# Two inner layers whose Gelu stays in its PSUM bank, with three smaller moves of order, in a macaron block with a long convolution

## The reference

```python
def _L0_ffn_ref(x, ...):                       # weights w1, w2, h1, h2, w3 hold -1, 0 or 1
    h = silu(_tlin(x, w1_w, w1_s)) * _tlin(x, w2_w, w2_s)      # 256 -> 1024
    h = gelu(_tlin(h, h1_w, h1_s), approximate=False)          # 1024 -> 1024
    h = gelu(_tlin(h, h2_w, h2_s), approximate=False)          # 1024 -> 1024
    return _tlin(h, w3_w, w3_s)                                # 1024 -> 256
...
x = x + 0.5 * ffn(layernorm(x))
x = x + attn(layernorm(x))                     # y = gelu(causal convolution with taps K); y @ W.T + b
x = x + 0.5 * ffn(layernorm(x))
```

## Time and profile before

| | us |
|---|---|
| median of 3 runs | 1358.97 (1357.96 to 1359.03) |
| profiled execution, own time | 1357.48 |
| its span in the trace | 1355.7 |
| PE busy | 1318.3 (97%) |
| DVE busy | 922.8 (68%) |
| ACT busy | 759.2 (56%) |
| POOL busy | 419.8 (31%) |

### The profile page before, as it was taken

One profiled execution on the slowest core, in us unless ns is written; L12 is line 12 of the kernel. 1 busy time (PEld: TensorE's weight loads), 2 busy tenths in 40 slices (PEclk: granted clock), 3 DMA queues, 4 the chain that ended last, 5 costly groups with the idle time before them and its releaser, 6 DMA issues.

```text
span 1355.7 us, 18622 instructions
## 1 busy us (share of the span) xinstructions
PE 1318.3 (97%) x7278; PEld 669.2 (49%) x7278; DVE 922.8 (68%) x1742; ACT 759.2 (56%) x1201; POOL 419.8 (31%) x354
## 2 busy tenths in 40 slices
PE   8999879999999999999999999999999999999997
PEld 3454344555544435455454554545545455454544
DVE  5376978832544886888878888789877883454723
ACT  5565247564447457474674746747467464545533
POOL 6822861200010442625326253262532610001000
PEclk9999989999999999999999999999999999999999
DMA  8210000000010000000000000000000002131400
GB/s 332 95 47 9 8 1 10 8 1 16 0 47 17 0 16 1 8 9 0 10 7 9 8 16 9 24 9 8 16 8 24 8 11 76 44 113 37 150 1 18
DMA packets 44703, 41.90 MB, mean 31 GB/s; under 512 B 32704, under 2 KB 41408, under 8 KB 41920
## 3 DMA queue, kind: packets, MB, share of 16 engines
q1 hardware_dynamic: 44608, 40.64, 10.0%
HBM read 28.57 MB, written 4.19 MB: 24 GB/s over the span
## 4 chain that ended last, share of the span: by engine, by line
PE 80%; DVE 15%; ACT 3%; issue 1%; DMA 1%; POOL 0%; SPq 0%; DVEq 0%; ACTq 0%; POOLq 0%
PE psf L1327 52%; PE psf L1315 14%; PE psf L1339 8%; DVE arena L786 4%; DVE hab L616 3%; DVE arena L789 3%; PE pss L1390 2%; PE pss L1400 2%; PE pss L1380 1%; PE pss L1355 1%; DVE xnp L675 1%; DVE arena L242 1%; PE pss L1370 1%; ACT ht L1098 1%; DVE arena L783 0%
## 5 line engine op out<-in xcount | busy, mean ns | idle before, releaser
L1327 PE MATMUL psf<-hab,wall 128*128 128x512 f16 x4096 | 893.0, 380 | 8.8 <-DVE hab L616 4.8
L1327 PEld LDWEIGHTS psf<-hab,wall 128*128 128x128 f16 x4096 | 399.1, 98 | 492.0 <-issue 9.3
L616 DVE SCALAR_TENSOR_TENSOR hab<-ht,hab 128x512 f16<-128x512 f32 x384 | 317.3, 831 | 286.8 <-ACT hab L1090 283.7
L1098 ACT ACTIVATE ht<-psf,scf 128x512 f32<-128x512 f32 x256 | 174.3, 681 | 411.0 <-PE psf L1327 398.7
L1090 ACT ACTIVATE hab<-ht 128x512 f16<-128x512 f32 x384 | 241.4, 629 | 28.8 <-DVE ht L627 20.4
L1315 PE MATMUL psf<-h,wall 128*128 128x512 f16 x1024 | 233.7, 381 | 17.8 <-ACT sil L1080 16.6
L1315 PEld LDWEIGHTS psf<-h,wall 128*128 128x128 f16 x1024 | 99.5, 98 | 135.4 <-ACT sil L1080 18.5
L954 POOL TENSOR_SCALAR rs<-mv 128x4 f32<-128x4 f32 x16 | 6.2, 389 | 493.7 <-DVE mv L658 487.5
L627 DVE SCALAR_TENSOR_TENSOR ht<-psf,scf,sil 128x512 f32<-128x512 f32 x128 | 95.9, 750 | 81.8 <-PE psf L1315 73.1
L1080 ACT ACTIVATE sil<-psf,scf 128x512 f32<-128x512 f32 x128 | 88.0, 687 | 86.0 <-PE psf L1315 83.9
L1339 PE MATMUL psf<-wall,hab 128*128 128x256 f16 x1024 | 117.0, 273 | 0.0
(11 more groups left out here) (127 smaller groups left out, 873.4 us busy)
## 6 DMA issues: line engine op xcount, KB each, us to landing
arena<-wh SPq DMA_DIRECT2D x8, 1024.0 KB, 5.5
g<-wh SPq DMA_DIRECT2D x6, 1024.0 KB, 10.1
out<-xr SPq DMA_DIRECT2D x15, 256.0 KB, 2.2
xr<-x SPq DMA_DIRECT2D x7, 512.0 KB, 5.1
arena<-w SPq DMA_DIRECT2D x3, 1024.0 KB, 5.3
g<-w SPq DMA_DIRECT2D x2, 1024.0 KB, 6.8
xr<-wh SPq DMA_DIRECT2D x2, 1024.0 KB, 10.3
g<-w SPq DMA_DIRECT2D x2, 512.0 KB, 6.1
```

What stands on the lines that cost most here:

```text
L616: e.scalar_tensor_tensor(out=hab[:, buffer(p), m, 1, :], in0=ht[:, p % 3, :], scalar=2.0 ** E2 if l else 1.0, in1=hab[:, buffer(p), m, 0, ...
L1098: e.activation(ht[:, p % 3, :], psf[bank_use(i, "hid", s) % MAIN][:, :], ACT.Gelu, scale=scf[:, 2 + l, m:m + 1]).then_inc(s_gelu, 1)
L1327: ins = e.matmul(bank[:, :], WH[:, l, m // 2, k, ms], hab[:, buffer(p), k, part, :], start=(k == 0 and part == 0), stop=(k == KH - 1 and p ...
```

## The change

There are five edits. (1) Gelu of an inner tile is written back to its own bank, and both splits read the bank; `ht` serves the gate's tiles alone. The bank is free for PE when the low half is done. (2) Tile 15 is split like the others, ahead of the first Silu and the first gate. (3) The factors' cast on ACT stands in slot 25 of pass 1, their low half on DVE in slot 7 of pass 2 (due from slot 3); four of the rounds of matmuls that use them, and the casts around them, move by two or three slots. (4) The bias is added by DVE in slot 14. (5) `BESIDE` is cut in slot 6 from 2700 to 2000 and in slot 14 from 2700 to 1500; `halves` is cut into pieces.

```diff
-BIAS_AT = 12
+BIAS_AT = 14
-BESIDE = [0, 500, 2000, 2700, 2700, 2700, 2700, 6800] + [0, 500, 2000, 2700, 2700, 2700, 2700, 1000]
+BESIDE = [0, 500, 2000, 2700, 2700, 2700, 2000, 6800] + [0, 500, 2000, 2700, 2700, 2700, 1500, 1000]
+FACTORS_HIGH_AT, FACTORS_LOW_AT = T(1, 25), T(2, 3)
@@ bank_free
             if s < 16:
-                return s_gelu, 2 * KH * i + s + 1
+                return s_lo, tile(i, 1, s) + 1
@@
+        def source(p):
+            i, s = divmod(p, 3 * KH)
+            return ht[:, (KH * i + s) % 3, :] if s < KH else psf[bank_use(i, "hid", s - KH) % MAIN][:, :]
@@ dve_program
-                    out=hab[:, buffer(p), m, 1, :], in0=ht[:, p % 3, :], scalar=2.0 ** E2 if l else 1.0,
+                    out=hab[:, buffer(p), m, 1, :], in0=source(p), scalar=2.0 ** E2 if l else 1.0,
@@
+            def bias_rows(b):
+                rows = xr[:, NB * b:NB * (b + 1), :]
...
+                e.tensor_tensor(rows, rows, bb[:, :].unsqueeze(1).to_broadcast([P, NB, D]), ALU.add).then_inc(s_xb, 1)
+                return 2300
@@
-                for s in range(2 * KH - 1):
+                for s in range(2 * KH):
                     split_low(tile(i, 1, s))
                     slot(i, s)
...
-                    behind = tile(i, 1, 2 * KH - 1)
+                    behind = tile(i + 1, 0, 0)
@@ act_program
-                w.wait_ge(s_lo, p - 2)
-                e.activation(ht[:, p % 3, :], psf[bank_use(i, "hid", s) % MAIN][:, :], ACT.Gelu,
-                             scale=scf[:, 2 + l, m:m + 1]).then_inc(s_gelu, 1)
+                e.activation(bank, bank, ACT.Gelu, scale=scf[:, 2 + l, m:m + 1]).then_inc(s_gelu, 1)
@@
-                yield At(mark["pj"][0] + 1)
+                yield At(FACTORS_HIGH_AT)
```

More of the change, by code:

```diff
@@ L624, in gate @@
                 w.wait_ge(s_silu, KH * i + m + 1)
-                if p >= 3:
-                    w.wait_ge(s_lo, p - 2)
+                g = KH * i + m - 3
+                if g >= 0:
+                    w.wait_ge(s_lo, tile(g // KH, 0, g % KH) + 1)
                 e.scalar_tensor_tensor(
-                    out=ht[:, p % 3, :], in0=psf[bank_use(i, "up", 2 * m + 1) % MAIN][:, :], scalar=scf[:, 1, m:m + 1],
+                    out=source(p), in0=psf[bank_use(i, "up", 2 * m + 1) % MAIN][:, :], scalar=scf[:, 1, m:m + 1],
                     in1=sil[:, m % 2, :], op0=ALU.mult, op1=ALU.mult).then_inc(s_gate, 1)
@@ L708, in taps, with factors_low @@
                 mark["pj"] = now["slot"], ch.n
-                yield At(now["slot"] + 1)
+            def factors_low():
+                yield At(FACTORS_LOW_AT)
                 for q in range(2):
@@ L722, in powers @@
                         yield time
-                    k = halves(ch, 1, n)
-                    yield 2 * (cost(qh[1][0][0]) + quick(qh[1][0][0]))
-                    mark["qlo", n] = now["slot"], k
+                    if not n:
+                        yield from factors_low()
+                    for time in halves(ch, 1, n):
+                        mark["qlo", n] = now["slot"], ch.n
+                        yield time
             def taps_low():
@@ L863, in fixed @@
                         time += y_low(u)
+                    if u % 2 and s == BIAS_AT:
+                        time += bias_rows(u // 2)
                     for half in range(2):
@@ L921, in dve_program @@
                 else:
-                    split_low(tile(i, 1, 2 * KH - 1))
-                    slot(i, 2 * KH - 1)
                     assert strand.over
@@ L989, in powers @@
                         yield 2.2 * time
-                    k = halves(ch, 0, n)
-                    yield 9000
-                    pmark["qlo", n] = now["slot"], k
+                    for time in halves(ch, 0, n):
+                        pmark["qlo", n] = now["slot"], ch.n
+                        yield 2.2 * time
             def first_products(u):
@@ L1089, in split_high @@
                     w.wait_ge(s_gate, KH * i + m + 1)
-                e.activation(hab[:, buffer(p), m, 0, :], ht[:, p % 3, :], ACT.Copy,
+                e.activation(hab[:, buffer(p), m, 0, :], source(p), ACT.Copy,
                              scale=2.0 ** E2 if l else 1.0).then_inc(s_hi, 1)
```

33 lines of the change are left out of this document (13 added, 20 removed).

## The result

| kernel | median | runs | ratio to before, 95% interval |
|---|---|---|---|
| before | 1357.96 us | 1356.23 to 1359.03 | |
| changed | 1351.33 us | 1349.34 to 1351.67 | 0.9948 [0.9934, 0.9963] |

The changed kernel is 6.6 us faster by the medians. The forecast was 1350.6, that is 8.35 less than the 1358.97 that was known then; the median of before is 1.0 lower here, so the time was met within 0.7 us and the gain was 1.7 smaller than forecast. Its profiled execution, the fastest of the five, took 1349.34 us with a span of 1347.6 and a mean clock of 0.994. The page of the changed kernel, to be read against the earlier trace rows: first the busy time of each engine, then the chain that ended last by engine.

What follows compares the result with a forecast made beforehand. PE bounds the kernel, busy 97% of the span, so only its idle time or low clock can be saved. Terms -2.3 + 1.6 - 1.1 - 4.25 - 1.1 - 1.2 = -8.35 took 1358.97 to 1350.6 us, range 1344.5 to 1358.

Steps and rivals of the forecast that it cites:

- Edit 3, -2.3: End of pass 1: moving the factors' cast shortens PE's 13.69 us stop; gain 1.0 to 3.5 us, taken as 2.3.
- The two stops forecast: End of pass 1: PE stops at 161.9 for tile 14's low half, again at 173.5 for the first gate.
- the last 6.4 us of factors: DVE in pass 1: factor work expected behind tile 14's low half, which would come at about 169.4.
- The rounds moved in pass 2, 0: Pass 2: moved rounds and the factors' low half cost nothing; 1 to 3 us once if the cover is gone.
- Edits 2 and 5 in pass 0, +1.6 and -1.1: Pass 0: a later first gate stops PE for 1.6 us; less strand in slot 23 gains 1.1 us.
- Edit 1: Inner low halves drop from 831 ns to 0.69 us with PSUM; pass 5 gains 4.25 us, pass 12 1.1.
- rival B: Inner splits: no gain from PSUM, since one input still comes from SBUF; 1357.2 us, chance 0.12.
- the 1.7 of clock: Pass 5: 1.8 us lost to half clock speed, expected to go together with the 2.46 us stop.
- Edit 4, -1.2: Ends of passes 6, 8, 10: the bias on DVE gains 0.4 us each, 1.2 in all (-3 to 2.9).
- the 0.96: PE stop in each of passes 6, 8, 10, expected to go, with 0.6 us waiting for DVE's first gate instead.
- rival C: Ends of passes 6, 8, 10, 12: DVE reaches the first gate late, costing 9.2 us; 1366.4 us, chance 0.10.
- Rival A: End of pass 1: the stop at 163.6 goes altogether, ACT being its only cause; 1337.6 us, chance 0.08.

## Why the prediction came out right, step by step

**Edit 3, -2.3: the size held, the cause did not.** Pass 1 gained 2.52 us. The forecast for DVE looks good at its end: the gate was to begin at 176.5 and began at 176.67; but counted from the pass's first matmul, which came 1.5 us later here, it began 1.4 us sooner than forecast. And the forecast named the wrong edit. With edit 3 undone the stop is the same; with edit 1 undone PE stopped for 13.37, and pass 1 took 93.24 (91.80 with edit 4 undone too, by a shorter stretch of low clock). In that kernel tile 12's low half took 1.12 and tile 13's 1.53 beside POOL, and the first gate began 1.9 us later, counted from the pass's first matmul. The gain of pass 1 is the splits', 2.5 to 3.9 us by how long the clock stays low; that it came out at the forecast 2.3 is luck. The two stops forecast were one: I put "the last 6.4 us of factors" behind tile 14's low half, for 169.4. The order has two products and a subtraction on either side of it. Those ahead took the 6.4 us; those behind took 2.1, when POOL had gone on to small instructions. So the low half came at 174.0 instead of 169.4 and everything waited once. The step that failed is that I took a duration that belonged to POOL's neighbour and carried it along with an instruction that moved.

**The rounds moved in pass 2, 0: wrong, 3.18.** I said that PE had no idle time there, and gave 1 to 3 us once as the price if the cover went. It went, for a reason that stood in the trace: DVE's powers of 4.04 and 2.50 us beside POOL, at 247.5 to 254 in the kernel before, came 7 us later in the pass, where by edit 1 the bank of tile 14 is held until the low half behind them. Holding POOL's halves back returned 2.0 of the 3.2; the rest are stops of 0.31 and less. No single edit makes the loss: the pass took 85.21 with edit 3 alone, 86.23 with edit 1 undone, and 87.73 with edit 3 undone (1.7 of it the clock's). The term that failed is the one put at nothing.

**Edits 2 and 5 in pass 0, +1.6 and -1.1: right.** The stop is 1.91 (forecast 1.6), the 1.25 at 103.9 is gone, and so is the 0.30 ahead of the up step, which I had not counted.

**Edit 1: right in its price, and rival B fell.** The mean of the 256 inner low halves is 687 ns, the maximum 693. Pass 5 gained 4.58 (4.25), of which edit 1 made 1.74 and the shorter strand 1.1; the 1.7 of clock was in the forecast, but it belongs to the one execution that was profiled (edit 3 alone: the same stop, no fall), so this term is right in part by luck. Pass 12: a stop of 0.59 where I had 0.5, and the later one is gone where I had left 0.75 of it.

**Edit 4, -1.2: too small, 3.84.** The first half was right: tile 8's low half ended 41.0 us into pass 6, forecast 41.8, before 48.1. Then I let DVE lose most of that lead again. The sums of y were to end 57.2 us in, and ended 54.5 in; the first gate was to begin at 63.3, and began at 60.2. DVE does 3.1 us more there and is still 2.5 us earlier than before. The mis-sized term is the backlog between tile 8 and the gate. I also watched the wrong path: the forecast waits for DVE's first gate, but the 0.96 hung on the first Silu, behind ACT's cast of y, which waits for `y_sums`; the bias and the low halves of y, which I counted against the gain, stand behind `y_sums` on DVE and hold up neither that cast nor the Silu. That also settles rival C: the lag was made by the slow low halves and the 4.9 us product, as I said against it.

**Rival A** (the stop goes altogether) had the wrong cause but a possible end: without POOL beside the factors the stop does go, and pass 1 is 12.5 us shorter; the kernel keeps that only if pass 2 doesn't take it back.

## What to carry to other kernels

Before costing a move, write beside each long instruction what ran on the other engine meanwhile: a duration stretched by a neighbour does not move with the instruction, and the neighbour may find another victim. Ask of every stop which engine's work is stretched, not only which is named: here ACT's 13 us wait, the cast and DVE's order were all on the way, and two waits that hold POOL back, with one slot of strand emptied, took the time from 1351.33 to 1334.36, more than twice what the whole change gained. Compare the same stop in two kernels before you call its cost a gain: a fall of the clock after it may be there in one execution and not in the next. And an order or a slot number on an engine without waits holds nothing in time.
